# Four attention blocks on one core: the third attention's scores computed once, work moved between VectorE, GpSimd and TensorE, and a new set-up

## The reference

```python
x = L0(ctx, x, mask)        # attention of x over [ctx, x], 16 heads of 16, masked; rmsnorm; 256-1024-256 MLP with gelu; residuals
x = L1(x, state=ctx)        # RWKV: token shift and mixing, projections r k v w g, a scan over the tokens, group norm, gate, channel mixing
x = L2(x, ctx)              # one-head attention over ctx, residual
x = L3(x, ctx, amask)       # attention over ctx, 32 query heads on 8 key heads of 8 channels, additive mask; residual, layer norm

# L1's scan, for each sequence and each of 32 heads of 8x8
out_t = r_t @ (u * k_t v_t^T + s);   s = k_t v_t^T + w_t * s

# L3's attention ("third attention" in the change; layer 1 in the code's own count, L0's being layer 0)
scores = einsum('bkgld,bksd->bkgls', q, k) / sqrt(8) + amask
out = softmax(scores) @ v
```

## Time and profile before

| what | value |
|---|---|
| median of 3 runs | 1760.15 us (1754.41 to 1763.23) |
| the profiled execution, own time | 1761.26 us |
| its span, first to last instruction | 1759.5 us |
| mean granted TensorE clock | 0.969 of full |
| TensorE busy | 1585.7 us, 90% |
| VectorE busy | 1105.4 us, 63% |
| ScalarE busy | 613.3 us, 35% |
| GpSimd busy | 500.5 us, 28% |

### The profile page before, as it was taken

One profiled execution on the slowest core, in us unless ns is written; L12 is line 12 of the kernel. 1 busy time (PEld: TensorE's weight loads), 2 busy tenths in 40 slices (PEclk: granted clock), 3 DMA queues, 4 the chain that ended last, 5 costly groups with the idle time before them and its releaser, 6 DMA issues.

```text
span 1759.5 us, 43483 instructions
## 1 busy us (share of the span) xinstructions
PE 1585.7 (90%) x18936; PEld 1180.5 (67%) x18936; DVE 1105.4 (63%) x1926; ACT 613.3 (35%) x1329; POOL 500.5 (28%) x492
## 2 busy tenths in 40 slices
PE   4687999999999999999999999999999999997765
PEld 3564777767777777777676776777777777765543
DVE  1246567665767776565766766576777656574732
ACT  1232343434234343433334343423434343331211
POOL 1023333323233332323233332323333232323310
PEclk8799999999999999999999999999999999998978
DMA  6002020201102020201102020100202020010100
GB/s 262 10 4 54 10 68 17 71 17 47 29 17 68 17 71 16 65 17 28 53 17 68 17 71 16 51 25 17 68 16 71 16 65 19 19 40 12 46 7 7
DMA packets 65533, 70.89 MB, mean 40 GB/s; under 512 B 19776, under 2 KB 54592, under 8 KB 64960
## 3 DMA queue, kind: packets, MB, share of 16 engines
q1 hardware_dynamic: 65344, 68.11, 13.3%
HBM read 30.33 MB, written 4.19 MB: 20 GB/s over the span
## 4 chain that ended last, share of the span: by engine, by line
PE 64%; DVE 21%; POOL 5%; issue 4%; ACT 3%; DMA 2%; SPq 0%; DVEq 0%; POOLq 0%; ACTq 0%
PE pw L396 27%; PE pw L377 8%; PE pw L371 8%; PE pw L583 6%; PE pw L577 5%; DVE mx L1054 5%; DVE ab L1180 2%; DVE tB L1093 2%; PE pw L689 2%; PE pw L382 2%; DVE ab L1176 1%; PE pw L504 1%; POOL ab L1013 1%; DVE ptC L1227 1%; DMA wb<-in_wb 1%
## 5 line engine op out<-in xcount | busy, mean ns | idle before, releaser
L1013 POOL TENSOR_TENSOR ab<-ab,kvrg 128x512 f32<-128x512 f32 x128 | 174.9, 1366 | 277.5 <-DVE ab L1180 277.5
L1180 DVE TENSOR_TENSOR_SCAN ab<-wS,ab 128x260 f32<-128x260 f32 x256 | 221.1, 904 | 5.9 <-ACT ab L908 1.5
L1054 DVE TENSOR_REDUCE mx<-pw 128x16 f32<-128x1024 f32 (+1 forms) x128 | 149.9, 1210 | 32.1 <-PE pw L396 31.8
L1006 POOL TENSOR_TENSOR big<-big,xaB 128x512 f32<-128x512 f32 x80 | 95.5, 1210 | 182.0 <-DVE big L1158 182.0
L371 PE MATMUL pw<-big,wb 128*128 128x256 f32 x512 | 127.8, 393 | 0.0
L577 PE MATMUL pw<-tA,wb 128*128 128x256 f32 x512 | 123.4, 391 | 0.7 <-DVE tA L1129 0.7
L583 PE MATMUL pw<-wb,ptA 128*128 128x256 f32 x512 | 118.6, 385 | 0.0
L862 ACT ACTIVATE ptA<-pw,wa 128x256 f32<-128x256 f32 x128 | 53.8, 471 | 165.6 <-PE pw L577 165.5
L371 PEld LDWEIGHTS pw<-big,wb 128*128 128x128 f32 x512 | 93.2, 192 | 23.2 <-issue 11.8
L577 PEld LDWEIGHTS pw<-tA,wb 128*128 128x128 f32 x512 | 95.9, 195 | 18.7 <-issue 5.5
L583 PEld LDWEIGHTS pw<-wb,ptA 128*128 128x128 f32 x512 | 94.8, 190 | 16.9 <-issue 5.2
(11 more groups left out here) (215 smaller groups left out, 3227.7 us busy)
## 6 DMA issues: line engine op xcount, KB each, us to landing
big<-kvrg SPq DMA_DIRECT2D x256, 128.0 KB, 2.4
hT<-in_h SPq DMA_DIRECT2D x16, 512.0 KB, 4.3
wb<-in_wb SPq DMA_DIRECT2D x1, 5120.0 KB, 23.6
...
```

The lines of the kernel that those rows point to most:

```text
L1006: G.tensor_tensor(v, v, xaB[:, :, :, 1:S + 1].rearrange("p k b s -> p (k b) s"), ALU.add).then_inc(xm_ok, 1)
L1013: G.tensor_tensor(ab[i % 4][:, :, :, 0:S], st[i % 2][:, :, :, 0:S], r, ALU.mult).then_inc(pd_ok, 1)
L1054: V.tensor_reduce(mx[:, 2 * j:2 * j + 2, g * p:g * p + g], pw[:, 2 * j:2 * j + 2, :].rearrange("p r (g s) -> p r g s", g=g), AXX, ALU.max) ...
L1180: last = V.tensor_tensor_scan(st[i % 2][:, j, :, :].rearrange("p b s -> p (b s)"), wS[:, i // 4, :, :].rearrange("p b s -> p (b s)"), ab[i ...
```

## The change

- The third attention's scores are computed once, with queries on the partitions. VectorE adds the mask (now a tile mq, line 1024's maximum with LEAST stays on GpSimd) while it copies the scores to SBUF (ms, which lies over pt[1]) and takes the maxima from there. GpSimd subtracts the maxima, ScalarE takes the exponentials in place, TensorE turns them block by block into banks 0 to 3, and ScalarE copies them back to SBUF over ms. turn1 has two halves now.
- k times v is on GpSimd (`outer`), one step ahead of the scan.
- The permuting product is gone: Wv's columns are permuted on the host so that v comes in the order of the sums, `copy_v` reads 16 neighbouring rows, and VectorE adds cv when it copies the sums out (in place of ScalarE).
- Set-up: rows is loaded earlier; the bias rows are folded in bank 4 first; the folding of L2's weights is done in the first tile's turn0, and what VectorE does for it in the first tile's max0 and norm0.
- ORDER is new, with 83 letters. Per iteration, from the end of the r projection on, it reads: pw2, pg, gate, ruk, scan 0, cv, scan 1, exp0.0, scan 2, fr, l2v, sum 0, scan 3, fv, scan 4, exp0.1, sum 1, scan 5, x2turn, l2s, value0.0, l2p, oturn.0, scan 6, l2o, k3, value0.1, v3, sum 2, out0.0, out0.1, scan 7, x3turn, norm0, q3, sum 3, oturn.1, zturn, max1.0, up.0, up.1, max1.1, up.2, up.3, turn1.0, gnorm.0 to .3, down.0, turn1.1, exp1.0, down.1, exp1.1, value1.0, gturn, value1.1, out1.0, norm1, outg, out1.1, norm3, norm2.

The diff, cut to its core:

```diff
-             ("top", P), ("dup", P), ("o3", 2 * C)]
+             ("top", P), ("o3", 2 * C)]
...
 def attention(layer):
-    return [... ("turn", 1), ("exp", 2), ("value", 2), ("out", 2)) for p in range(ps)]
+    return [... ("turn", 1 + layer), ("exp", 2), ("value", 2), ("out", 2)) for p in range(ps)]
...
-ORDER = "AABAACBABCCBACACCBBABCBAACBAACABCBBBABBBCCBBBCACBBCABBBCBBAABCBCABBBBCBBACBCACBCCB"
+ORDER = "AABAACBBBACBBCABBBBBBBBBBBBABCCBBCBABBCCACBBCCACBAABCACBBACAACAACBBBBACCACCBCCABCCB"
...
-        m3 = sb("m3", [P, NB, S])
+        mq = sb("mq", [P, NB, S])
+        ms = ptC[:, :].rearrange("p (i r n) -> p i r n", i=2, r=4)
...
             def copy_v(q):
-                    src = vS[2 * jp + i::J, m, :].unsqueeze(1).broadcast_to([HT, J, NT])
+                    j = 2 * jp + i
+                    at = 32 * (j % 4) + HT * (j // 4)
+                    src = vS[at:at + HT, m, :].unsqueeze(1).broadcast_to([HT, J, NT])
...
-                elif name == "exp1" and i == 1 and t + 1 < TILES:
-                    sp.wait_ge(e_ps, 2 * TURN[1, t] + 2)
+                elif name == "turn1" and i == 1 and t + 1 < TILES:
+                    sp.wait_ge(am_ok, t * 4 + 4)
                     load_mask(t + 1)
...
             load_keep(0)
+            sp.dma_start(rows[:, :, :], rows_d...).then_inc(ld_rows, 16)
             load_x(0, a1, ld_x1)
             load_x(0, xB[0], ld_x4[0])
             sp.dma_start(ptC[:, 0:nn], nat_d).then_inc(ld_nat, 16)
-            sp.dma_start(rows[:, :, :], rows_d...).then_inc(ld_rows, 16)
             sp.dma_start(wb[:, :], wb_d).then_inc(ld_wb, 16)
...
             def max_scores(layer, p):
-                            into(ps[r][:, 256 * i:256 * i + 256], q3T..., kz3..., i == 0, False)
+                            last = into(ps[r][:, 256 * i:256 * i + 256], q3T..., kz3..., i == 0, i == 1)
...
-                    else:
-                        for r in BY_HALF:
-                            last = into(ps[r]..., w("dup")[half(r), :], m3[half(r), b, :]..., False, i == 1)
...
-            def exp_scores(layer, p):
+            def exp_scores(p):
...
             def gather(t, p):
-                if a == 1:
-                    last = into(out[:, 0:NT], w("perm"), cv[:, m, :], False, True)
...
+            def fold_weights():
+                pe.wait_ge(ld_nat, 16)
+                pe.wait_ge(set_b, 1)
+                for m in range(2):
+                    for k in range(2):
+                        mm(kn(b4)[:, m, :], nat[:, 1, k, m * P:(m + 1) * P], nat[:, 0, k, :], start=(k == 0), stop=(k == 1))
+                    for k in range(2):
+                        last = mm(kn(b5)[:, m, :], nat[:, 2, k, m * P:(m + 1) * P], nat[:, 3, k, :], start=(k == 0), stop=(k == 1))
+                last.then_inc(set_pe, 1)
...
             def part_a(name, i, t):
+                if t == 0 and name == "turn0":
+                    fold_weights()
...
                 elif name == "xturn":
                     if t:
                         pe.wait_ge(x1_ok, t)
+                    else:
+                        pe.wait_ge(set_m, 1)
...
                 elif name == "sum":
-                    if i == 1:
+                    if i == 2:
                         pe.wait_ge(cv_ok, t + 1)
...
                 elif name == "max1":
-                        pe.wait_ge(m3_ok, t + 1)
                     else:
-                        pe.wait_ge(a_mx, 4 * a + 2)
+                        pe.wait_ge(am_ok, t * 4 + 2)
                     max_scores(1, i)
-                elif name == "turn1":
-                    pe.wait_ge(a_mx, 4 * TURN[1, t] + 4)
-                    nc.tensor.transpose(ps[0][:, 0:P], mx..., ident).then_inc(mt_ps, 1)
                 elif name == "exp1":
-                    exp_scores(1, i)
+                    for j in range(2):
+                        pe.wait_ge(ex_ok, t * 4 + 2 * i + j + 1)
+                        if i == 0:
+                            pe.wait_ge(am_ok, t * 4 + 2 + j + 1)
+                        else:
+                            pe.wait_ge(e_sb, 4 * TURN[1, t] + j + 1)
+                        for r in (2 * j, 2 * j + 1):
+                            for c in range(4):
+                                last = nc.tensor.transpose(ps[r][:, tok(c)], ms[:, i, r, tok(c)], ident)
+                        last.then_inc(ex_ps, 1)
...
 @@ TensorE, before its first stage @@
-            pe.wait_ge(ld_nat, 16)
...
-                    mm(kn(b4)[:, m, :], nat[:, 1, k, m * P:(m + 1) * P], nat[:, 0, k, :], start=(k == 0), stop=(k == 1))
...
             pe.wait_ge(ld_w, 16)
             for k in range(2):
-                mm(kn(ps[3])[:, 0, :], vec("vb0", k).broadcast_to([P, P]), w("o0", k), start=(k == 0), stop=(k == 1))
+                mm(kn(b4)[:, 0, :], vec("vb0", k).broadcast_to([P, P]), w("o0", k), start=(k == 0), stop=(k == 1))
...
-            pe.wait_ge(set_m, 1)
             pe.wait_ge(set_pool, 2)
             pe.wait_ge(set_dve, 5)
...
 @@ ScalarE @@
-                elif name == "oturn":
-                    act.wait_ge(rd_ps, t * 4 + 2 * i + 2)
-                    A(oT[:, i, :], (b4, b5)[i][:, 0:NT], ACT.Copy).then_inc(ot_sb, 1)
...
                 elif name == "turn1":
-                    A(mT[:, :], ps[0][:, 0:P], ACT.Copy).then_inc(mt_sb, 1)
+                    for j in range(2):
+                        act.wait_ge(su_ok, t * 4 + 2 * i + j + 1)
+                        A(ms[:, i, 2 * j:2 * j + 2, :], ms[:, i, 2 * j:2 * j + 2, :], ACT.Exp).then_inc(ex_ok, 1)
                 elif name == "exp1":
-                    weights(1, TURN[1, t], i)
+                    for j in range(2):
+                        act.wait_ge(ex_ps, t * 4 + 2 * i + j + 1)
+                        A(pt[1][i][:, 2 * j:2 * j + 2, :], pw[:, 2 * j:2 * j + 2, :], ACT.Copy).then_inc(e_sb, 1)
...
 @@ GpSimd @@
+            def outer(t, i):
+                pool.wait_ge(vx_ok[i % 3], (t * (3, 3, 2)[i % 3] + i // 3 + 1) * 32)
+                if i >= 4:
+                    pool.wait_ge(rd_ps, t * 4 + i // 2 - 1)
+                k = kS[:, i // 4, :]....broadcast_to([P, 2, NB, S])
+                G.tensor_tensor(ab[i % 4][:, :, :, 1:S + 1], vx[i % 3]..., k, ALU.mult).then_inc(a_ok, 1)
...
+                elif name == "ruk":
+                    outer(t, 0)
                 elif name == "scan":
+                    if i + 1 < 8:
+                        outer(t, i + 1)
                     pool.wait_ge(sc_ok, t * 8 + i + 1)
...
+                elif name == "turn1":
+                    for j in range(2):
+                        pool.wait_ge(a_mx, 4 * TURN[1, t] + 2 * i + j + 1)
+                        for r in (2 * j, 2 * j + 1):
+                            v = ms[:, i, r, :].rearrange("p (g s) -> p g s", g=8)
+                            last = G.tensor_tensor(v, v, mx[:, r, 8 * i:8 * i + 8].unsqueeze(2).broadcast_to([P, 8, S]), ALU.subtract)
+                        last.then_inc(su_ok, 1)
...
 @@ VectorE @@
+            def fold_rows():
+                dve.wait_ge(ld_rows, 16)
+                dve.wait_ge(set_pe, 1)
+                V.tensor_tensor(rows[:, ROWS.index("out_b"), :], rows[:, ROWS.index("out_b"), :], kn(b4)[:, 0, :], ALU.add)
+                V.tensor_tensor(rows[:, ROWS.index("bo"), :], rows[:, ROWS.index("bo"), :], kn(b4)[:, 1, :], ALU.add).then_inc(set_b, 1)
+
+            def fold_weights():
+                dve.wait_ge(ld_wb, 16)
+                for k in range(2):
+                    V.tensor_scalar(w("blk", k), w("blk", k), vec("u", k), None, ALU.mult)
+                dve.wait_ge(set_pe, 2)
+                V.tensor_scalar(flat(m_qk[:, :, :]), b4[:, :], 1.0 / 16.0, None, ALU.mult)
+                V.tensor_scalar(flat(m_vo[:, :, :]), b5[:, :], vec("alpha"), None, ALU.mult).then_inc(set_m, 1)
...
             def part_a(name, i, t):
+                if t == 0 and (name, i) == ("max0", 1):
+                    fold_rows()
+                if t == 0 and (name, i) == ("norm0", 0):
+                    fold_weights()
...
+                elif name == "oturn":
+                    dve.wait_ge(rd_ps, t * 4 + 2 * i + 2)
+                    dve.wait_ge(cv_ok, t + 1)
+                    V.tensor_tensor(oT[:, i, :], (b4, b5)[i][:, 0:NT], cv[:, i, :], ALU.add).then_inc(ot_sb, 1)
                 elif name == "scan":
-                    dve.wait_ge(vx_ok[i % 3], ...)
-                    if i >= 4:
-                        dve.wait_ge(rd_ps, t * 4 + i // 2 - 1)
-                    V.tensor_tensor(ab[i % 4][:, :, :, 1:S + 1], vx[i % 3]..., k, ALU.mult).then_inc(a_ok, 1)
...
                 elif name == "max1":
-                    maxima(1, TURN[1, t], i)
+                    dve.wait_ge(a_ps, 2 * TURN[1, t] + i + 1)
+                    dve.wait_ge(m3_ok, t + 1)
+                    for r in range(4):
+                        last = V.tensor_tensor(ms[:, i, r, :]..., ps[r]..., mq[:, 2 * i:2 * i + 2, :]..., ALU.add)
+                        if r % 2:
```

(10 more changed lines are left out.)

115 lines of the change are left out of this document (37 added, 78 removed).

## The result

The kernel after takes 1712.8 us (median of 4 runs, 1708.2 to 1713.7) beside 1758.5 for the kernel before: a ratio of 0.973, 95% interval 0.970 to 0.977. It is faster, as forecast, inside the range, and 33 us slower than the forecast of 1680. The profiled execution took 1713.5, its span is 1711.7.

What follows compares the result with a forecast made beforehand. TensorE was taken to bound full iterations, chains the ends. Start -17, A and B -5, full iterations -45, B and C -5, last iteration -9 sum to -81, giving 1680 us; range 1610 to 1735.

Steps and rivals of the forecast that it cites:

- 36 less 28.6 and 3 us: Full iteration: scan stretch lasting 36 us for 28.6 of TensorE work, plus 3 us idle in the first third.
- The start: Start of the run: first product no longer waits for the folding chain, net -17 us (bounds -20 and -12).
- The -22 of the earlier q projection: Start: TensorE's first product comes at about 10.5 us instead of 32.34, -22 us.
- The +5 for the foldings in the queue: Start: folding ahead of turn0 on TensorE, row additions and scalings ahead on VectorE, +5 us (bounds 2 and 8).
- the 14 full iterations: Iterations running parts A, B and C: each 97.2 us instead of 100.4, or -3.2; fourteen give -45 us.
- A and B: Iteration with parts A and B only: scan waits less but steps are longer, -5 us (bounds -10 and +5).
- B and C: Iteration with parts B and C only: -5 us, bounds -10 and +5.
- C alone: Last iteration: third attention's first scores to first value product 17.5 instead of 26.5 us, -9 (bounds -12 and -5).
- the second place to look at: ScalarE's PSUM copies queue behind second-half exponentials, which wait for GpSimd's last subtraction; at most +4.8 us of copies, forecast hidden.
- Cover holds: Rival, scan steps: scans fit beside GpSimd's products, step 2.4 us, iteration 92.7, total 1617; chance 0.28 (1590 to 1650).
- The scan chain slower: Rival, eight scan steps: chain bounds the iteration, 7 to 8 us per us of step, slower above 4.2; chance 0.08.
- The end of C late: Rival, exp1 or value1: late GpSimd subtractions make TensorE wait 2 us, iteration 99.5, total 1712; inside the range.

Runs made afterwards that it cites:

- k_times_v_vector: The kernel after with the product k times v back on VectorE for all eight scan steps, new order kept: 1681.5 us, ratio 0.956 to the kernel before.
- writes_only: The kernel after with GpSimd's product k times v left out, two constant fills of the same buffer in its place: 1638.1 us, ratio 0.932 to before.
- fill_five_waits: The kernel after with 20 unused TensorE products ahead of the five waits of the scan stretch: 1730.1 us, ratio 0.982 to before.
- old_set_up: The kernel after with the weight foldings back ahead of the first q projection: 1737.4 us, ratio 0.989 to before.
- k3_before_l2p: The kernel after with k times v on VectorE and the third attention's key product k3 moved ahead of l2p: 1667.3 us, ratio 0.946 to before.

## Why the prediction was right and where it was off

**The sign and the mechanism were right.** TensorE's work falls to 87.3 us in a full iteration at full clock (359.0 to 456.4; forecast 87.0). The turnings cost 4.4, my lower bound, where the sum has 5.3; some 1.5 us, spread over the other groups, took that gain back. The step with k times v on GpSimd is 3.05 to 3.44 (forecast 3.35, and 3.65 with every instruction blocked to its end), and k_times_v_vector and writes_only show that its cause is the exclusion. GpSimd has 50.7 us in that iteration (forecast 53): its subtractions cost 1.04 and not 1.36, while the product k times v is blocked most of the time and costs 1.56 in the mean. VectorE has 73.1 (forecast 69 to 70): I had costed its scans at the old price, and the blocked ones take 70 us more over the run, 4.4 a tile. Idle time of TensorE in that iteration is 10.1 us (forecast 10): sum 0 2.0 and sum 1 1.5 (forecast 0.9 and 2.1), l2s, l2p and oturn 0 3.4 (forecast 3.5). An iteration takes **97.3 to 97.5 where its clock stays up or drops briefly; the forecast was 97.2**. The forecast's own terms give 97.0 with its rounded 10 us, or 97.4 with 36 less 28.6 and 3 us.

**The start** gave -21.6 (forecast -17). The -22 of the earlier q projection measured -21.0. The +5 for the foldings in the queue was wrong: they run from 30.07 to 34.1, beside the reduction that turn0 waits for (30.19 to 32.5), and their price is about 1.5 us, which the rest of the iteration gets back.

**What failed is a term that I never priced: TensorE's clock.** I treated each wait as worth its own length. The forecast for the 14 full iterations was -45, measured is -27.8. Five of them are 3.0 to 3.5 us longer with a fall of about 7 us in the clock, 15 of the missing 17; the other 2 are 97.4 instead of 97.2 in each. The other falls, of some 3.4 us, cost 0.1 at most in this kernel: the value products slow down where TensorE would have waited at l2p anyway. fill_five_waits shows that the falls go when the waits go. The Trainium skill ("TensorE: Matmul & The Clock Gate", section "HAM oscillation — how this bites in real kernels") describes a kernel in which a wait for a DMA lowers the clock in every round. Here a fall comes back in 11 of the 14 full iterations, so the trace agrees on the repetition; but it follows several waits of 0.8 to 2.0 us, each shorter than those of the page. I should have weighed that rule against the idle time that I had myself forecast.

**A and B** (forecast -5, measured +2.4) and **B and C** (-5, measured +5.8) are within the bounds for the first and a little outside for the second. Both missed in good part by the clock again. old_set_up has the same stages there and needs 3.6 us less for each. B and C of the kernel before, A and B of the kernel after, then both stretches of old_set_up:

```profile
1587.00:1677.00 90.00, 69.82 (x691) 47.79 (x689) 55.26 (x101) 21.98 (x52) 26.67 (x24) 0.87 0.11 29
```
```profile
73.11:161.76 88.65, 68.22 (x618) 50.59 (x617) 48.75 (x80) 25.41 (x56) 35.09 (x31) 0.85 0.19 29
```
```profile
94.45:179.50 85.05, 65.76 (x618) 48.61 (x617) 48.75 (x80) 25.42 (x56) 35.11 (x31) 0.88 0.19 30
1565.50:1657.20 91.70, 62.02 (x428) 42.38 (x428) 61.25 (x101) 25.13 (x53) 46.47 (x40) 0.80 0.17 28
```

At 0.88 instead of 0.85, A and B takes 85.05 instead of 88.65; at 0.80 instead of 0.75, B and C takes 91.7 instead of 95.4. In B and C TensorE was busy for 69.8 us before and is for 66.4 now, though a tile has 9.2 less of its work: by that estimate, the clock took 5.8 us in all. The engine of k times v decides less there: with it on VectorE, B and C takes 91.4 in k_times_v_vector at a clock of 0.78, but 95.5 in k3_before_l2p at 0.73. The rest is the forecast's own mechanism, longer steps against a shorter queue: with the clock of old_set_up the two stretches would be -1.2 and +2.2 beside the kernel before, not -5 each. **C alone**: -6.8 (forecast -9); 19.4 us from the first scores to the first value product (forecast 17.5), as turnings cost 3.65 to 3.97 there at the low clock and the first of the last ones waits 3.73 for ScalarE, the place that the forecast had named as the second to look at.

The sum: start 4.6 better, A and B 7.4 worse, full iterations 17, B and C 10.8, C 2.2 worse; together 33.

**The rivals.** *Cover holds* is out: beside a product k times v hardly any scan pair escapes (2 of 112 take under 1.4 us). It came near in writes_only (iterations of 93.0 to 95.9, forecast 92.7), where GpSimd's second operation doesn't read. *The scan chain slower* is out too, and its rate (7 to 8 us an iteration for each us of a step) was far too steep: 0.3 to 0.7 us on the early steps is worth 1.2. *The end of C late* came near in time (1712), but by luck: its wait at exp1 or value1 in a full iteration is not what made them longer, and its own 2 us would give 99.2 and 1708, not 99.5 and 1712.
